# A decoder layer on one core: orders of all engines written anew, the residual sums of three batches as identity products, 13 warm-up products

## The reference, cut to what matters

```
x = layernorm(x + attn(x))     # linear attention, 16 heads of 8: elu+1 features of q and k, k normalised,
                               # scores = q k^T, out = scores v, @ Wo + bo; y = x + out; layernorm(y)*gamma + beta
x = layernorm(x + xattn(x, context))   # 16 heads of 64 over 64 context rows: softmax(q k^T / 8) v @ Wo
x = layernorm(x + ffn(x))      # fp4_linear(silu(fp4_linear(x, w_gate)) * fp4_linear(x, w_up), w_down), 352 wide
# fp4_linear: both operands cut in blocks of 16, scaled by the block's max/6, rounded to the E2M1 grid, scaled back
```

## Time and profile before

| what | value |
|---|---|
| median of 3 runs | 372.65 us (372.3 to 372.66) |
| profiled execution, its own time | 374.35 us |
| its span on the core | 372.6 us |
| granted TensorE clock, mean | 0.996 |
| busy: TensorE / VectorE / ScalarE / GpSimd | 351.0 / 307.9 / 253.4 / 269.1 us |

### The profile page before, as it was taken

One profiled execution on the slowest core, in us unless ns is written; L12 is line 12 of the kernel. 1 busy time (PEld: TensorE's weight loads), 2 busy tenths in 40 slices (PEclk: granted clock), 3 DMA queues, 4 the chain that ended last, 5 costly groups with the idle time before them and its releaser, 6 DMA issues.

```text
span 372.6 us, 7321 instructions
## 1 busy us (share of the span) xinstructions
PE 351.0 (94%) x2143; PEld 268.7 (72%) x2143; DVE 307.9 (83%) x858; ACT 253.4 (68%) x533; POOL 269.1 (72%) x453
## 2 busy tenths in 40 slices
PE   7999998999998999999999999999999999998874
PEld 6688655775775968778678867786777788887663
DVE  2798756658689998869989779979998998999994
ACT  2757867586677678668687767868767656864553
POOL 4403549967988689969779895898989569784535
PEclk9999999999999999999999999999999999999998
DMA  7900100001000001000000000000000000000010
GB/s 251 300 2 16 30 1 14 16 16 29 15 17 14 2 15 43 16 30 17 15 29 14 17 1 17 28 3 0 17 15 2 15 2 0 8 23 14 3 30 28
DMA packets 13586, 10.44 MB, mean 28 GB/s; under 512 B 971, under 2 KB 12396, under 8 KB 13548
## 3 DMA queue, kind: packets, MB, share of 16 engines
q1 hardware_dynamic: 12540, 7.89, 7.0%
q10 hardware_dynamic: 1008, 2.10, 1.7%
HBM read 7.88 MB, written 2.10 MB: 27 GB/s over the span
## 4 chain that ended last, share of the span: by engine, by line
PE 71%; POOL 8%; DVE 8%; issue 6%; ACT 5%; DMA 1%; POOLq 0%; ACTq 0%; DVEq 0%
PE A L2860 13%; PE S L2833 12%; PE TP L2823 7%; PE F L2879 6%; PE TP L2851 6%; PE A L2895 5%; PE A L2784 3%; PE S L2842 3%; PE TP L2762 2%; POOL pe L431 2%; PE S L2762 2%; PE F L2762 2%; PE TP L2888 2%; PE A L2797 2%; DMA wqkT<-in_wk_t 1%
## 5 line engine op out<-in xcount | busy, mean ns | idle before, releaser
L431 POOL TENSOR_TENSOR pe<-pe,srec 128x1024 f32<-128x1024 f32 x32 | 60.9, 1904 | 9.2 <-DVE srec L1835 8.9
L2833 PE MATMUL S<-M,x1T 128*128 128x512 f32 x128 | 60.7, 597 | 1.5 <-ACT pe L1064 1.4
L2860 PEld LDWEIGHTS A<-wvoT,wqkT 128*128 128x128 f32 x480 | 56.4, 192 | 3.1 <-issue 1.8
L2860 PE MATMUL A<-wvoT,wqkT 128*128 128x128 f32 x480 | 58.0, 276 | 0.1
L425 POOL TENSOR_TENSOR fold<-pe 128x512 f32<-128x512 f32 x32 | 40.8, 1276 | 14.5 <-ACT pe L1064 14.2
L1818 DVE TENSOR_REDUCE smax<-S 128x16 fp32r<-128x1024 f32 x32 | 38.7, 1210 | 3.2 <-PE S L2833 3.1
L1064 ACT ACTIVATE pe<-S 128x1024 f32<-128x1024 f32 x32 | 32.6, 1020 | 10.6 <-PE S L2842 10.3
L1069 ACT ACTIVATE wqkT<-TP 128x1024 f32<-128x1024 f32 x32 | 32.6, 1019 | 4.3 <-PE TP L2851 4.1
L2833 PEld LDWEIGHTS S<-M,x1T 128*128 128x128 f32 x128 | 22.2, 190 | 18.3 <-issue 15.3
L2879 PE MATMUL F<-w_gu_r,xf_r 128*128 128x352 f32 x168 | 35.0, 344 | 0.1
L2851 PE MATMUL TP<-ident,pe 128*128 128x128 f32 x256 | 33.5, 274 | 1.6 <-POOL pe L431 1.0
(11 more groups left out here) (247 smaller groups left out, 890.2 us busy)
## 6 DMA issues: line engine op xcount, KB each, us to landing
xT<-in_x_t SPq DMA_DIRECT2D x16, 128.0 KB, 2.1
x_sb<-in_x SPq DMA_DIRECT2D x16, 128.0 KB, 2.1
out<-yf SPq DMA_DIRECT2D x15, 128.0 KB, 1.8
M<-in_fw SPq DMA_DIRECT2D x1, 560.0 KB, 11.0
wqkT<-in_wq_t ACTq DMA_DIRECT2D x2, 256.0 KB, 4.5
wqkT<-in_wk_t ACTq DMA_DIRECT2D x2, 256.0 KB, 5.8
ctx_f<-in_ctx_t ACTq DMA_DIRECT2D x2, 256.0 KB, 6.9
wvoT<-in_wv_t ACTq DMA_DIRECT2D x1, 512.0 KB, 9.2
```

The source lines that it names most:

```text
L431: ge.tensor_tensor(w, w, spread(srec[n % 2][:, :], HX, R), ALU.mult).then_inc(pn_made, 1)
L2833: last = te.matmul(S[:, half * BANK:half * BANK + BANK], x1T[b % 2][:, t * P:t * P + P], M[:, b // BH, HC * half:HC * half + HC, b % BH * ...
L2860: last = te.matmul(A2[:, t * P:t * P + P], pT[n % 2][:, j, :], vo[b % 2][:, j, :], start=(j == 0), stop=(j == NJ - 1))
```

## The change

No step of a batch goes or comes on any engine but these. On VectorE cross_residual, xf_cut_high, xf_keep_low and ffn_residual of batches 13 and 14 and the two tile_ffn_residual of batch 15 are left out. In their place `cross_out` of 13 and 14, `down` of 13 and 14 and `tile_down` start with a product of the identity with x1 or x2, which puts the residual into the bank; statistics and normalisation then read the bank. Batches 13 and 14 multiply `gate_up` unsplit in float32 from a whole xfT. `tile_down` of tile 1 writes bank A1 in place of A2. WARM is 13. The fillers are other ones: 14 in F0 ahead of gate_up(11, 0), 3 in TP0 ahead of h_transpose(12), 12 in A2 ahead of tile_xf_transpose(15, 1), 6 in TP0 ahead of h_transpose(14) and 6 in A2 ahead of tile_down(15, 0), for 7 and 14 in TP0. And the tables of all five engines are written in another order, some 700 steps of which the diff shows a few lines.

```diff
+        xf_r = [GT[:, k, 0:2 * T, :].rearrange("p (s t) n -> p s (t n)", s=2) for k in range(2)]
+        xfT = several("xfT", 2, [P, T * P])
...
+        WHOLE_GATE = (13, 14)
+        SUM_ON_PE = (13, 14)
+        TILE_SUM_ON_PE = True
...
+        DN_OF = (A2, A1) if TILE_SUM_ON_PE else (A2, A2)
...
-        WARM = 8
+        WARM = 13
...
             def ffn_norm(b, t):
-                norm("ffn", b, t, yf[b % 2][:, t, :], yf[b % 2][:, t, :])
+                if b in SUM_ON_PE:
+                    wait_free(act, out_stored[b % 2], 16 * (b // 2))
+                norm("ffn", b, t, yf[b % 2][:, t, :], part(DN, t) if b in SUM_ON_PE else yf[b % 2][:, t, :])
...
             def keep_xfT(b):
-                act.wait_ge(xf_cut_made, b + 1)
-                sc.activation(xf_r[b % 2][:, 0, :], xf_cut[:, :], ACT.Copy).then_inc(xfT_kept, 1)
+                if b in WHOLE_GATE:
+                    act.wait_ge(xfT_made, b + 1)
+                    sc.activation(xfT[b % 2][:, :], A2[:, 0:T * P], ACT.Copy).then_inc(xfT_kept, 1)
+                else:
...
             def statistics(n, b):
+                if b in SUM_ON_PE and n == "cross":
+                    y = tiles(A2[:, 0:T * P])
+                    dve.wait_ge(o_made, T * b + T)
+                elif b in SUM_ON_PE and n == "ffn":
+                    y = tiles(DN[:, 0:T * P])
+                    dve.wait_ge(dn_made, b + 1)
...
             def cross_out(b, t):
+                if b in SUM_ON_PE:
+                    pe.wait_ge(x1_made, T * b + T)
+                    te.matmul(part(A2, t), ident[:, :], x1[b % NA][:, t, :], start=True, stop=False)
...
             def gate_up(b, t):
+                if b in WHOLE_GATE:
+                    for m, bk in enumerate(ffn_banks(b)):
+                        last = te.matmul(bk[:, 0:I], part(xfT[b % 2], t), w_gu[:, m, :], start=True, stop=True)
+                    last.then_inc(gu_made, 1)
+                    return
...
             def down(b):
+                    if b in SUM_ON_PE:
+                        pe.wait_ge(x2_made, T * b + T)
+                        te.matmul(blocks(part(DN, t), NBX), ident[:, :], x2[b % 3][:, NBX * t:NBX * t + NBX, 0:BLK],
+                                  start=True, stop=False)
...
             def tile_down(b, t):
+                if TILE_SUM_ON_PE:
+                    pe.wait_ge(x2_made, T * b + t + 1)
+                    te.matmul(blocks(part(DN_OF[t], t), NBX), ident[:, :], x2[b % 3][:, NBX * t:NBX * t + NBX, 0:BLK],
+                              start=True, stop=False)
...
+            pe.wait_ge(hg4_made, 11)
+            keep_warm(F0, 14)
+            gate_up(11, 0)
...
+            pe.wait_ge(normed["ffn"], 28)
+            keep_warm(A2, 12)
+            tile_xf_transpose(15, 1)
...
+            pe.wait_ge(normed["ffn"], 30)
+            keep_warm(A2, 6)
+            tile_down(15, 0)
```

More of the change, by code:

```diff
@@ new lines, in _ @@
+            k_features(11)
+            score_max(8, 0)
+            q_features(10)
+            gate_times(3, 1)
+            attn_residual(9)
+            statistics("attn", 9)
+            aggregate("attn", 9)
+            gated(3, 1)
+            h_max(3)
+            score_sums(8, 0)
+            h_reciprocal(3)
+            score_reciprocals(8, 0)
+            h_scaled(3)
+            score_max(8, 1)
+            h_rounded_up(3)
+            cross_residual(7)
+            h_rounded(3)
+            statistics("post", 9)
@@ L2536, in _ @@
[L2536 to L2550 removed]
+            xf_cut_high(9)
+            x_scaled(10)
@@ L2555, in _ @@
             statistics("ffn", 8)
-            score_max(13, 0)
+            x_rounded_up(10)
+            x_rounded(10)
+            aggregate("ffn", 8)
+            gate_times(9, 1)
+            gated(9, 1)
+            h_max(9)
+            h_reciprocal(9)
+            statistics("post", 14)
+            aggregate("post", 14)
+            h_scaled(9)
+            score_sums(13, 1)
+            score_reciprocals(13, 1)
+            h_rounded_up(9)
+            cross_residual(12)
+            h_rounded(9)
@@ new lines, in _ @@
+            x_reciprocal(12)
+            x_scaled(12)
+            gate_times(11, 0)
+            gated(11, 0)
+            score_reciprocals(14, 1)
+            x_rounded_up(12)
+            score_max(15, 0)
+            ffn_residual(10)
+            x_rounded(12)
+            aggregate("ffn", 9)
+            statistics("ffn", 10)
+            aggregate("ffn", 10)
+            gate_times(11, 1)
+            gated(11, 1)
+            h_max(11)
+            h_reciprocal(11)
+            h_scaled(11)
@@ L3236, in _ @@
+            kv_project(8)
             pe.wait_ge(vo_kept, 8)
             h_transpose(2)
-            kv_project(8)
+            attn_out(8)
+            scores_shift(6, 1)
+            pe.wait_ge(fq_made, 10)
+            down(2)
+            pe.wait_ge(pe_made, 14)
+            x1_transpose(7)
+            pe.wait_ge(hT_kept, 3)
+            p_transpose(6, 0)
+            pe.wait_ge(yf_made, 3)
+            xf_transpose(3)
+            pe.wait_ge(x1T_kept, 8)
+            scores(7, 0)
+            pe.wait_ge(xf_low_made, 4)
@@ new lines, in _ @@
+            gate_up(4, 0)
+            kv_project(10)
+            pe.wait_ge(xf_low_made, 5)
+            project_q(11)
+            attn_out(10)
+            pe.wait_ge(h_made, 9)
+            gate_up(4, 1)
+            pe.wait_ge(pe_made, 18)
+            x1_transpose(9)
+            pe.wait_ge(vo_kept, 10)
+            h_transpose(3)
+            pe.wait_ge(x1T_kept, 10)
+            scores(9, 0)
+            pe.wait_ge(fq_made, 12)
+            down(3)
+            scores_shift(9, 0)
+            pe.wait_ge(yf_made, 4)
```

2811 lines of the change are left out of this document (1366 added, 1445 removed).

## The result

The changed kernel takes 388.86 us (median of four runs, 387.59 to 390.19) against 372.65 before: a ratio of 1.0437, interval 1.039 to 1.0483, or 16.2 us slower. The direction was forecast, at 2.8 us; the size lies far outside the range of 369.0 to 379.0. The four runs fall in two pairs (387.59 and 387.74, 389.98 and 390.19), and the profiled execution is one of the upper pair: 390.19 us, with a span of 388.4, 15.8 more than before.

What follows compares the result with a forecast made beforehand. TensorE's list was taken to bound the kernel up to 343.8 us, then an FFN chain over all engines. The terms -1.5 + 7.0 - 4.0 + 1.3 = +2.8 us gave 375.4 us, range 369.0 to 379.0.

Steps and rivals of the forecast that it cites:

- The start, -1.5: Kernel start: 13 warm-up products for 8 let the first product and batch 0's k/v projection run faster, -1.5 us.
- the 6.6 named as the sign: Kernel start: the 13 warm-up fillers ended by 6.6 us, the 16 records after them taking 1.2 us.
- The rival of a warm-up that does nothing: Kernel start: the first product after the gap still takes 2.08 us, +1.5 us; no chance of its own given.
- TensorE's list up to the mark, +7.0: Up to the last attention product's end (343.8 us before): added products, unsplit gate_ups and 17 fillers lengthen TensorE's work, +7.0 us.
- Idle time gained, -4.0: Behind 44 us, up to the last attention product: larger distances between steps cut TensorE's 9.0 us idle, -4.0 us.
- The fillers, priced at 0.22 to 0.235 us each: TensorE's filler products counted at full-clock length, such as 14 taking 3.29 us and six 1.4 us.
- Behind the mark, +1.3: FFN chain after the last attention product: -2.7 earlier h_rounded(14), +3.2 bank A2 held, +0.8 VectorE standing, +1.3 us.
- The FFN sums' mechanism: Behind the last attention product: A2 frees only after ScalarE's normalisation, so tile_down(15, 0) waits; +3.2 us, six fillers included.
- The fillers hurt twice: Fillers in F delay batch 11's tanh and gate, 2 us, and batch 15 tile 1 pays whole: 378.6 us, chance 0.14.
- idle and filling time over 5 us to the last attention product: Sign for the forecast: TensorE idle or filling 5 us or more from 44 us to the last tile_cross_out.
- both waits on yf: Sign: TensorE waits twice on ScalarE's yf ahead of the A2 fillers, 2 us or more each.
- the mark near 345: Sign for the forecast: the last tile_cross_out, the last attention product, ends near 345 us.

Runs made afterwards that it cites:

- g3: The kernel before, in its own orders, with the FFN residuals of 14 and both tiles of 15 as identity products: 375.99 us (1.008).
- h2: The change with fillers ahead of their waits, without the other 9 (3 ahead of h_transpose(12), 6 ahead of h_transpose(14)): 378.56 us (1.0161).
- h1: The change without fillers, FFN residuals back on VectorE, then 14 fillers ahead of gate_up(11,0) and 12 ahead of tile_gate_up(15,1): 378.12 us (1.0137).

## Why the prediction was right and wrong

- **The start, -1.5: wrong in its cause.** The profile shows the rows that were forecast: the 16 records in 1.16 us, scores(0, 0) at 49.80 for 51.72. But g3, with 8 products, has its scores(0, 0) at 49.72. The one profile of before had caught the slower of two starts, and the step read a property of one execution as one of the kernel. By the ratio 13 products are worth 0.2 us (interval 0.9979 to 1.0008), that is nothing clear of noise. In the profile of that run they end at 7.36, not by the 6.6 named as the sign, and scores(0, 0) comes at 50.53, where it is 49.64 with 10 products. That is luck in part: in other profiles the same 26 records took between 4.53 and 5.92 us, and in h2 they ended at 6.36. The rival of a warm-up that does nothing was right in the median. The forecast quoted the Trainium skill (TensorE: Matmul & The Clock Gate, Part 1), that how much runs slow varies from run to run, and added that no run here shows it; by that rule, the trace agrees: 2.08 against 1.16 us behind the same 16 records.
- **TensorE's list up to the mark, +7.0: right.** Busy time up to the mark rises from 331.6 to 341.0, +9.4. Of this 2.1 are the ten more warm-up records (5.92 us for 3.78), which I had booked at the start. Of the 7.3 that remain, 1.7 are the 14 fillers at the lower level (5.02 us for 3.29), and 0.9 came off with the faster projections, so the steps as counted are worth some 6.5.
- **Idle time gained, -4.0: the step that failed first.** Measured: -0.1 (12.25 to 12.15), and behind 44 us, where the term was booked, +0.8 (9.0 to 9.8). The distances did bring what was claimed, -4.4 up to 250 us, 0.9 of them in the first 44. What was not seen is the other side: from 250 to the mark 4.3 us of new waits, 3.2 of them ahead of gate_up(11, 0). I wrote that VectorE can't let TensorE run freely, and took it as a limit of the gain, not as a source of a loss. I also booked VectorE 3.9 us less work. Its busy time rose by 2.0 instead, and by 5.5 with the orders alone (313.4 us, with the same 858 operations), though the mean of each of its costliest groups is the same within 3%. So it is the new order and not the operations; why, no run here shows.
- **The fillers, priced at 0.22 to 0.235 us each: wrong where it matters.** I saw that the 14 stand behind a wait and can only follow it, and then gave them their full-clock length. The clock falls soon behind such a wait, and the fillers are what runs then. All of them cost 5.5 us; ahead of the waits they gain 4 (379.11 against 383.21).
- **Behind the mark, +1.3: measured +6.5.** h_rounded(14) ends 13.95 us behind the mark, forecast 13.3. From there to the end of the last down it is 16.8 us (367.05 to 383.87) where the sum had 11.7. Of the 5.1, 3.3 lie ahead of the end of down(14), at 375.7 where 5.4 us behind h_rounded(14) is 372.4: the 12 fillers had held up gate_up of tile 1 and all behind it, and the 6 in TP0 stood between that gate_up and h_transpose(14) for another 1.3 us. VectorE stood 3.50 us for the tanh of tile 1, where the forecast had 0 to 2. And 1.6 are the 6 fillers (2.34 from start to start, for 1.4) and the last downs (2.67 for 2.0), in part at the lower level. What lies between, statistics, GpSimd and normalisation, came as worked out, 3.1 us for 2.9.
- **The FFN sums' mechanism: right, their price too low.** A2 held by ScalarE's normalisation costs 3.0 us in the kernel before and 3.7 in the new order. Of the +3.2 forecast 1.4 were six fillers, which neither of these has, so +1.8 is what compares. In g3 it is 11.2 us from h_rounded(14) to the end of the last down, where the sum without fillers had 10.3; 0.7 of the difference are the last six products at the lower level.
- **The rivals.** "The fillers hurt twice" named the right two places, and priced them at 3.2 us on top. Of the signs, idle and filling time over 5 us to the last attention product, both waits on yf and over 15 us from h_rounded(14) to the end (21.3) came; the mark near 345 did not (353.1), nor the second wait of 2 us (1.55).

## What to carry to other kernels

Price a wait of TensorE with what stands behind it. A wait of some 3 us that a new order makes cost its length here and then half the speed of products behind it, and fillers helped only where they stood ahead of the wait, in a bank that is free, where no cost of theirs shows: in the kernel before, 14 products cost 2.9 us behind a wait and saved 2.6 ahead of it, both against none. Profile the kernel before more than once, or look at how its times group, before a gain is claimed from one slow row; and let a warm-up end as the data arrives.

## What the hardware showed that was not expected

- After waits of 3.31, 3.64 and 4.29 us the products behind ran at half rate (1.51 us for 0.88, 2.90 for 1.58, 3.75 for 1.88), the granted clock being 0.50 to 0.70 in the stretches of 5 us that hold them. After one of 2.22 us in g3 the first six products of down took 0.83 us and the next six 1.49. In one kernel, h2, waits of 1.7, 1.1 and 0.9 us stood near the end and the clock read 1.00 throughout. The length of the wait just before does not decide it: in h1 the same h_transpose stands behind the same wait and runs slow. Here is h1, then h2:

```profile
363.07 1.51 PE L2924 MATMUL TP<-ident,hv 128*128 128x128 f32 x6 [1.70 <-POOL hv L452]
```

```profile
363.13 0.84 PE L2918 MATMUL TP<-ident,hv 128*128 128x128 f32 x6 [1.70 <-POOL hv L450]
```

- One and the same program starts at either level. Behind the same 16 records the next 16 took 2.08 or 1.16 us, and the times of the kernel before lie in two groups, round 372.3 and 373.7, half of the runs in each. The Trainium skill (TensorE: Matmul & The Clock Gate, Part 1) has the throttled state as the default, released by activity; the rows of the start agree: 16 records of 128 columns take 3.78 us there, 28 take 3.29 later on. The clock of the profile reads 1.00 in both places, so at the start only the durations show the lower level.
- A mean granted clock near one does not mean that little was lost: the changed kernel had 0.984 and took 388.4 us, its version without fillers 0.974 and 381.6. The fillers that ran slow did bring the clock back sooner at one place: behind the second wait the version without them reads 0.50 from 362 to 372 us, the changed kernel from 366 to 369. Behind the first wait both are back at 1.00 by 315. In all, the fillers cost more than that clock was worth.
